# Moving score products into the feed-forward steps of a fused attention and feed-forward kernel

## The chip, the cores and the metric

The kernel runs on one core of a Trainium2 chip. The metric is device time in microseconds (us) of one execution; lower is better. The engines are PE (TensorE, matrix products; its weight loads are listed as PEld), DVE (VectorE), ACT (ScalarE), POOL (GpSimd) and SP (SyncE, which here only issues DMAs). Each engine runs its own list of instructions in order and waits on semaphores. TensorE's clock has two levels, 1.2 and 2.4 GHz; the profile gives the granted clock as a share of the full level, so 0.50 is the lower one.

## The reference

Eight batches of 256 rows by 512 columns pass through two blocks.

```
x = x + attention1(causal_conv(x))           # 16 heads of 32, causal, ALiBi; qkv 512 -> 1536
u = attention2(x)                            # cond2: the 512 columns are the positions, 256 rows the channels
    Q, K, V = W x ;  att = Q K / 4 + b       # 16 heads of 16, 512 x 512 scores a head, masked keys
    y = softmax(att) V
x = x + ffn(y)                               # gate, up 512 -> 2048, down 2048 -> 512
    inter = silu(y Wg) * (y Wu);  out = inter Wd
```

The feed-forward weights are Catmull-Rom splines of few control points. Everything is fp32; products that need it are split into a high and a low part that run through TensorE's faster fp32r path.

## The kernel before

The work is written out by hand as one ordered list for each engine; `batch(b)` appears in each of them, with counts of semaphores (`wait("name", n)`) between engines. Batch 0 stands alone, batches 1 to 6 are a hardware loop, batch 7 stands alone again, and the feed-forward part of the last batch follows by itself.

The feed-forward part of batch b-1 is carried inside batch b. A batch has these stages on PE: scores, softmax and values of attention1; its projection; the queries, keys and values of attention2 (L955, L960); the **feed-forward window**; the **loop over j** of attention2; then the next batch's first values (L835).

**Feed-forward window.** Eight steps n (`NT` = 8), each over 256 of the 2048 inner columns. PE does `moments(n+1)` (L846, y against a table, into bank 2 or 7), `gate_up(n)` (L857) and `down(n-1)` (L868 to L870, 12 products that accumulate in banks 5 and 6, its weights in a ring of `RING` = 3 buffers that SP refills with 1 MB DMAs, L269). ACT does `z_copy(n+1)` (L518), Silu (L529) and a rounded copy (L534). DVE does `gated(n)` (L662) and `rest(n)` (L667). `down(n)` needs `rest(n)`.

**Scores of attention2.** 64 products of 52 x 512 (L977, `scores(s)`), 16 for each of 4 groups of heads, alternate between banks 0 and 1. DVE takes the maximum of each row (L741, `maximum(s)`), and `scores(s)` waits for `maximum(s-2)`. After a group's 16 maxima, `turn(g)` transposes them on PE (L990), DVE negates and splits them (L748, L751), and `max_rows(g)` issues four small DMAs on ACT's queue (L568) that put them as extra rows into `q2`. Only then can the shifted scores of that group run. 24 scores are in the window (`WINDOW_SCORES`): four in each of steps 4 to 7, then eight behind step 7. Their order in a step:

```
PE   moments(n+1), two scores, gate_up(n), two scores, down(n-1)
DVE  gated(n), two maxima, rest(n), two maxima
```

`turn(0)` follows step 7. The operands of the scores, `stack2_g`, are written by 12 DMAs of 64 KB for each group (`stacks2(g)`, L351), between which SP also issues the ring's loads.

**Loop over j.** 35 steps. Step j does `shifted(j)` (L1009, two products of 54 x 512; exp on ACT follows, L592), two of the remaining 40 scores while j < 20, and `values2(j-3)` (L1021, eight products of 128 x 256 with 32 columns each). At `TURN_AT` (j = 4, 12, 20) comes `turn(g)`; at `OUT_AT` (11, 19, 27) `turn_outputs` (L1033), after ACT has brought a group's result out (L575); at `QK1_AT` (j = 20 to 27) eight products each (L829) for the next batch's queries and keys. `shifted(1)` waits for `totals` (L674, DVE adds the feed-forward result to the residual), because it writes a bank of that sum. `shifted(8g)` waits for `max_rows(g)`.

**Values of attention2.** V is left in banks 0, 1, 6 and 7 (L960); DVE copies it out (L734) behind the splitting of queries and keys. `moments(1)` and the first scores wait for these copies, since they use the same banks.

Of the kernel before, what the change touches and what calls it, by code (L numbers as in the profile page):

```python
# [59 lines left out]
WINDOW_FROM = 4  # L60
WINDOW_SCORES = 24
# [12 lines left out]
def window_scores(n):  # L74
    return max(0, min(GS, 4 * (n - WINDOW_FROM + 1))) if n < NT else WINDOW_SCORES

# [34 lines left out]
def block_program(nc, x_lanes, x_rows, taps, conv_b, qkv_wT, qk_b, v_b, out_wT, out_b, slopes, cond, w2T, att_b,  # L111
# [7 lines left out]
    with ExitStack() as ctx:  # L119
# [59 lines left out]
        d_rows = sb("wd_rows", [P, IT], I32)  # L179

# [61 lines left out]
        def _(sp):  # L242
# [22 lines left out]

# [54 lines left out]
            def batch(b, first=False, last=False):  # L320
# [39 lines left out]
                for g in range(NG):  # L360
                    stacks2(g)
                    for n in range(RING + g, RING + g + 1 if g < NG - 1 else NT):
                        if not first:
                            load_weights(b, n)
                    for n in (2 * g, 2 * g + 1):
                        if first:
# [132 lines left out]
        def _(act):  # L499
# [36 lines left out]
            def batch(b, first=False, last=False):  # L536
# [25 lines left out]
                def max_rows(g):  # L562
                    wait("max2_high", g + 1)
                    wait("max2_low", g + 1)
                    for i, part in enumerate((max2_h, max2_l)):
                        for e in range(2):
                            row = e * ROWS2 + MAX2 + i
                            act.dma_start(q2[row:row + 1, g, :, :].rearrange("p h (t n) -> p (h t) n", t=CT),  # L568
                                          part[e * 2 * CT:(e + 1) * 2 * CT, g % 2, :]).then_inc(S["max2_rows"], 16)
# [14 lines left out]
                max_rows(0)  # L584
                for j in range(NP):
# [11 lines left out]
                    if j in TURN_AT:  # L597
                        max_rows(TURN_AT.index(j) + 1)
# [18 lines left out]
        def _(dve):  # L617
# [59 lines left out]
            def batch(b, first=False, last=False):  # L677
# [39 lines left out]

                wait("mask_loaded", 48)
# [8 lines left out]

                if first:
                    dve.wait_ge(gate_up_step, 3 * N_GEN)
                    nc.vector.memset(v2[:], 1.0).then_inc(ones_made, 1)  # L730
                    dve.wait_ge(ones_made, 2)
# [36 lines left out]
                for n in range(NT):  # L768
                    if first:
# [3 lines left out]
                    else:  # L773
                        gated(b, n)
                    had, now = window_scores(n - 1), window_scores(n)
                    for s in range(had, (had + now) // 2):
                        maximum(s)
                    if not first:
                        rest(b, n)
                    for s in range((had + now) // 2, now):  # L780
                        maximum(s)
                turn(0)
                for s in range(GS, WINDOW_SCORES):
                    maximum(s)
# [39 lines left out]
        def _(pe):  # L824
# [14 lines left out]
            def moments(b, n):  # L839
# [21 lines left out]
            def down(b, n):  # L861
                pe.wait_ge(S[f"w_loaded_{n % RING}"], fed(b, f"w_loaded_{n % RING}", 16 * (n // RING + 1)))
                pe.wait_ge(S["inter_low"], fed(b, "inter_low", n + 1))
                for s in range(LT):
                    for g in range(2):
                        lhs = (slice(None), n % 2, g, slice(s * P, (s + 1) * P))
                        w_h, w_l = stack1[:, n % RING, 0, g, :], stack1[:, n % RING, 1, g, :]
                        nc.tensor.matmul(psum[:, SUM_BANK + s, :], r(inter_h[lhs]), r(w_h), start=n + g == 0, stop=False)  # L868
                        nc.tensor.matmul(psum[:, SUM_BANK + s, :], r(inter_h[lhs]), r(w_l), start=False, stop=False)  # L869
                        last = nc.tensor.matmul(psum[:, SUM_BANK + s, :], r(inter_l[lhs]), r(w_h), start=False,  # L870
                                                stop=n == NT - 1 and g == 1)
                last.then_inc(S["down_step"], 1)

            def batch(b, first=False, last_batch=False):
# [105 lines left out]
                def turn(g):  # L980
# [3 lines left out]
                    elif g == 0:  # L984
                        pe.wait_ge(S["z_out"], fed(b, "z_out", NT))
                    elif g == 1:
                        wait("max2_low", 1)
                    else:
                        wait("y_out", g - 1)
# [36 lines left out]
                def turn_outputs(g):  # L1026
                    wait("o2_out", g + 1)
                    if g < NG - 1:
                        wait("max2_low", g + 2)
# [6 lines left out]
                if first:  # L1036
                    pe.wait_ge(fixed2, 64)
                    for s in range(GS):
                        scores(s)
                    turn(0)  # L1040
                    for s in range(GS, WINDOW_SCORES):
                        scores(s)
                else:
# [3 lines left out]
                    for n in range(NT):  # L1047
                        had, now = window_scores(n - 1), window_scores(n)
                        if n == 0:
                            wait("v2_out", CT)  # L1050
                        if n + 1 < NT:
                            moments(b, n + 1)
                        for s in range(had, (had + now) // 2):
                            scores(s)
                        if n == 0:
                            wait("k2_out", LT)
                        gate_up(b, n)
                        for s in range((had + now) // 2, now):
                            scores(s)
                        if n:  # L1060
                            down(b, n - 1)
                    turn(0)
                    for s in range(GS, GS + 2):
                        scores(s)
                    down(b, NT - 1)
                    for s in range(GS + 2, WINDOW_SCORES):
                        scores(s)
# [51 lines left out]
            moments(B, 0)  # L1119
            for n in range(NT):  # L1120
                if n + 1 < NT:
                    moments(B, n + 1)
                gate_up(B, n)
                if n:
                    down(B, n - 1)
            down(B, NT - 1)
# [148 lines left out]
```

## Time and profile before

| | us |
|---|---|
| three runs | 1688.45, 1693.24, 1705.03 |
| median | 1693.24 |
| profiled execution, its own time | 1703.24 |
| span of the profiled execution | 1701.4 |

| engine | busy us | share of the span |
|---|---|---|
| PE | 1414.6 | 83% |
| PEld | 783.8 | 46% |
| DVE | 774.7 | 46% |
| ACT | 509.6 | 30% |
| POOL | 350.6 | 21% |

The mean granted clock of TensorE is 0.854 of full speed. A busy PE may be busy at the lower level, where the same product takes about twice as long. The device time of the profiled execution is 1.84 us more than its span.

### The profile page before, as it was taken

The page shows a single profiled execution, that of the slowest core. Times are in us where ns is not written, and L with a number is a line of the kernel's source. Part 1 is how long each engine was busy: PE and PEld are TensorE (multiplying, and loading weights), DVE is VectorE, ACT ScalarE, POOL GpSimd, SP SyncE. Part 2 cuts the span into 40 slices and gives each one's busy share as a digit, 9 for nine tenths or more (in the row PEclk, how much of TensorE's full clock was granted, in tenths as well). Part 3 has the DMA queues.
Part 4 walks back from the last instruction along what each step waited for, and adds up shares of the span by engine and source line. Part 5 has one row for each costly group of instructions (what it writes and reads, how often), then busy time and mean ns, then how long its engine had stood idle before and what let it go on. Part 6 is the DMA issues. An engine that isn't in the chain of part 4 may idle for free.

```text
span 1701.4 us, 23331 instructions
## 1 busy us (share of the span) xinstructions
PE 1414.6 (83%) x8680; PEld 783.8 (46%) x8680; DVE 774.7 (46%) x1205; ACT 509.6 (30%) x652; POOL 350.6 (21%) x203
## 2 busy tenths in 40 slices
PE   4571698888988899888988889888998889898988
PEld 3240245453555435454454534554355544555435
DVE  5344634446244553535435362544525354343622
ACT  2021253214412243222432135122432224331352
POOL 3289103410052100801026100521008010000000
PEclk9795599986898869986899869998699877998679
DMA  9767312550335303361034602353033610345203
GB/s 301 236 188 238 106 36 68 149 157 18 69 109 128 119 2 88 118 162 57 13 78 140 178 18 60 105 134 126 2 88 114 163 61 2 88 136 165 101 1 136
DMA packets 80495, 181.12 MB, mean 106 GB/s; under 512 B 14404, under 2 KB 54292, under 8 KB 70708
## 3 DMA queue, kind: packets, MB, share of 16 engines
q1 hardware_dynamic: 76304, 174.68, 35.1%
q0 software_dynamic: 1280, 4.20, 1.0%
q8 instruction: 82, 1.34, 0.3%
q10 hardware_dynamic: 2816, 0.79, 0.2%
q14 instruction: 13, 0.11, 0.0%
HBM read 106.41 MB, written 21.14 MB: 75 GB/s over the span
## 4 chain that ended last, share of the span: by engine, by line
PE 63%; DVE 14%; issue 6%; ACT 6%; POOL 4%; DMA 3%; ACTq 3%; SPq 1%; DVEq 0%; POOLq 0%
PE psum L1021 9%; PE psum L829 7%; PE psum L977 6%; PE psum L1009 6%; PE psum L868 5%; PE psum L870 4%; PE psum L869 4%; PE psum L857 3%; PE psum L846 3%; DVE max L741 3%; PE psum L835 3%; ACTq L568 3%; ACT probs L592 2%; PE psum L946 2%; PE psum L911 2%
## 5 line engine op out<-in xcount | busy, mean ns | idle before, releaser
L741 DVE TENSOR_REDUCE max<-psum 128x1 f32<-128x512 f32 x512 | 329.6, 685 | 121.7 <-PE psum L977 120.4
L592 ACT ACTIVATE probs<-psum 128x1024 f32<-128x1024 f32 x256 | 255.6, 1023 | 262.7 <-PE psum L1021 191.9
L977 PE MATMUL psum<-k,q 52*128 52x512 f32 x512 | 204.3, 580 | 117.3 <-DVE max L741 102.7
L1021 PE MATMUL psum<-probs,v 128*32 128x256 f32 x2048 | 205.7, 488 | 18.9 <-ACT o L575 14.0
L977 PEld LDWEIGHTS psum<-k,q 52*128 52x128 f32 x512 | 103.0, 243 | 202.5 <-DVE max L741 170.7
L1009 PE MATMUL psum<-q,k 54*128 54x512 f32 x512 | 168.7, 625 | 23.3 <-ACT probs L592 16.4
L662 DVE TENSOR_TENSOR probs<-psum,probs 128x512 f32<-128x512 f32 x64 | 44.3, 692 | 243.6 <-ACT probs L529 243.6
L829 PE MATMUL psum<-h,qkv_w 128*128 128x256 f32 x512 | 133.5, 408 | 18.2 <-DVE h L627 18.0
L479 POOL TENSOR_TENSOR h<-h_in,tap 128x1024 f32<-128x1024 f32 x7 | 13.3, 1901 | 643.6 <-PE psum L835 643.5
L1009 PEld LDWEIGHTS psum<-q,k 54*128 54x128 f32 x512 | 62.4, 231 | 150.8 <-issue 85.0
L868 PE MATMUL psum<-stack 128*128 128x512 f32 x256 | 123.1, 481 | 2.0 <-DVE stack L667 2.0
L489 POOL TENSOR_TENSOR h<-h,products 128x1024 f32<-128x1024 f32 x49 | 121.8, 2486 | 3.8
L829 PEld LDWEIGHTS psum<-h,qkv_w 128*128 128x128 f32 x512 | 98.1, 201 | 52.5 <-issue 25.3
L554 ACT ACTIVATE probs<-psum 128x1024 f32<-128x1024 f32 x64 | 62.2, 1022 | 196.2 <-PE psum L932 196.2
L870 PE MATMUL psum<-stack 128*128 128x512 f32 x256 | 115.7, 452 | 0.0
L869 PE MATMUL psum<-stack 128*128 128x512 f32 x256 | 115.1, 450 | 0.0
L486 POOL TENSOR_TENSOR products<-h_in,tap 128x1024 f32<-128x1024 f32 x49 | 99.2, 2025 | 3.0
L518 ACT ACTIVATE z<-psum 128x256 f32<-128x256 f32 x64 | 24.4, 381 | 233.2 <-PE psum L846 233.2
L1021 PEld LDWEIGHTS psum<-probs,v 128*32 128x32 f32 x2048 | 47.2, 121 | 101.8 <-issue 60.5
L846 PE MATMUL psum<-y,z_table 128*32 128x256 f32 x1024 | 73.2, 408 | 24.9 <-DVE v L734 24.1
L646 DVE CAST high<-low 128x1024 fp32r<-128x1024 f32 x32 | 26.6, 830 | 145.7 <-ACT low L505 109.5
L707 DVE RECIPROCAL inv<-psum 128x256 f32<-128x256 f32 x32 | 56.2, 1758 | 68.6 <-PE psum L911 67.8
(103 smaller groups left out, 1777.8 us busy)
## 6 DMA issues: line engine op xcount, KB each, us to landing
stack<-wd_sorted SPq DMA_DIRECT2D x64, 1024.0 KB, 5.9
stack<-high SPq DMA_DIRECT2D x128, 128.0 KB, 2.4
stack<-low SPq DMA_DIRECT2D x64, 128.0 KB, 2.4
q<-high SPq DMA_DIRECT2D x128, 64.0 KB, 4.7
k<-high SPq DMA_DIRECT2D x128, 64.0 KB, 2.6
wd_sorted<-stack SPq DMA_DIRECT2D x8, 1024.0 KB, 5.0
h_in<-in_x_lanes SPq DMA_DIRECT2D x9, 512.0 KB, 5.0
x<-in_x_rows SPq DMA_DIRECT2D x8, 512.0 KB, 5.6
```

Source lines behind the costliest of these rows:

```text
L486: nc.gpsimd.tensor_tensor(products[:], h_in[:, :, k:k + L], over(tap[:, :, k:k + 1]), ALU.mult)\
L489: nc.gpsimd.tensor_tensor(h[:], h[:], products[:], ALU.add).then_inc(S["conv_step"], 1)
L592: nc.scalar.activation(probs[:, u // 2 % 2, u % 2 * 2:u % 2 * 2 + 2, :], psum[:, 2 + u % 2 * 2:4 + u % 2 * 2, :], ACT.Exp)\
L741: nc.vector.reduce_max(max2[:, g, e, i, t:t + 1], psum[:, s % 2, :], AX_X).then_inc(S["s2_max"], 1)
L829: last = nc.tensor.matmul(psum[:, o % 2, 0:L], qkv_w[:, c, o * P:(o + 1) * P], h[:, c, :], start=c == 0, stop=c == CT - 1)
L846: last = nc.tensor.matmul(psum[s * ZR:(s + 1) * ZR, Z_BANKS[n % 2], 0:L], zt[:, c, cols], y[:, c, :], start=i == 0, stop=i == 1, skip_grou ...
L868: nc.tensor.matmul(psum[:, SUM_BANK + s, :], r(inter_h[lhs]), r(w_h), start=n + g == 0, stop=False)
L869: nc.tensor.matmul(psum[:, SUM_BANK + s, :], r(inter_h[lhs]), r(w_l), start=False, stop=False)
L870: last = nc.tensor.matmul(psum[:, SUM_BANK + s, :], r(inter_l[lhs]), r(w_h), start=False, stop=n == NT - 1 and g == 1)
L977: nc.tensor.matmul(psum[:, e, :], r(q2[rows, g, i, t * P:(t + 1) * P]), r(k2[rows, g, i, :]), start=True, stop=True).then_inc(S["s2_ready" ...
L1009: last = nc.tensor.matmul(psum[:, 2 + u % 2 * 2 + e, :], r(k2[rows, g, u % 2, kt * P:(kt + 1) * P]), r(q2[rows, g, u % 2, :]), start=True, ...
L1021: last = nc.tensor.matmul(psum[e * BLK:(e + 1) * BLK, 6, queries], v2[:, kt, head, :], probs[:, kt % 2, e, queries], start=kt + half == 0, ...
```

## The change

The scores move forward and change their place in a step. `WINDOW_FROM` goes from 4 to 1, and `WINDOW_SCORES` is now 4 x (8 + 1 - 1) = 32: four in each of steps 1 to 7 and four in a new step 8, which holds only `down(7)`. `down` is cut into its two halves of six products. In a step:

```
PE   moments(n+1), two scores, gate_up(n), [turn(0) at n = 5], down(n-1) half 0, two scores, down(n-1) half 1
DVE  two maxima, gated(n), [turn(0) at n = 5], two maxima, rest(n)
```

From these constants follow `TURN_AT` = 0, 8, 16 and `QK1_AT` = 16 to 23; `OUT_AT` stays. The loop keeps 32 scores, two a step while j < 16. `moments(7)` waits until `turn(0)` has been read out of bank 7.

`max_rows` goes from ACT's queue to SP's: group 0 behind the next mask's load, groups 1 to 3 behind the store of the output. SP now issues `stacks2(1)` before it waits to refill the ring, and then loads 3; 4 and 5; 6 and 7 behind groups 1, 2 and 3. V is copied out by ACT, in front of the feed-forward part, no longer by DVE. Two activations of one element each (`warm`) stand where they make ACT load its table: Silu ahead of the queries, Exp behind the feed-forward part. The memset of `v2` in batch 0 moves ahead of the splits.

```diff
-WINDOW_FROM = 4
-WINDOW_SCORES = 24
+WINDOW_FROM = 1
+WINDOW_SCORES = 4 * (NT + 1 - WINDOW_FROM)
+TURN_STEP = WINDOW_FROM + GS // 4
...
+def window_pair(n, i):
+    first = 4 * (n - WINDOW_FROM) + 2 * i
+    return range(first, first + 2) if n >= WINDOW_FROM else ()
...
+            def max_rows(b, g):
+                sp.wait_ge(S["max2_high"], at(b, "max2_high", g + 1))
+                sp.wait_ge(S["max2_low"], at(b, "max2_low", g + 1))
+                for i, part in enumerate((max2_h, max2_l)):
+                    for e in range(2):
+                        row = e * ROWS2 + MAX2 + i
+                        sp.dma_start(q2[row:row + 1, g, :, :].rearrange("p h (t n) -> p (h t) n", t=CT),
+                                     part[e * 2 * CT:(e + 1) * 2 * CT, g % 2, :]).then_inc(S["max2_rows"], 16)
...
-                    for n in range(RING + g, RING + g + 1 if g < NG - 1 else NT):
-                        if not first:
-                            load_weights(b, n)
+                    else:
+                        for n in ((), (3,), (4, 5), (6, 7))[g]:
+                            load_weights(b, n)
...
                     load_mask(cond[b])
+                max_rows(b, 0)
...
                     sp.dma_start(out[b - 1], x_res).then_inc(S["out_stored"], 16)
+                for g in range(1, NG):
+                    max_rows(b, g)
...
+                if not first:
+                    nc.scalar.activation(warm[:], ones[:, 0:1], ACT.Silu)
...
+                for t in range(CT):
+                    wait("v2_ready", t + 1)
+                    nc.scalar.activation(v2[:, t, :, 0:DH],
+                                         psum[:, V2_BANKS[t], 0:L].rearrange("p (h d) -> p h d", h=H2), ACT.Copy)\
+                        .then_inc(S["v2_out"], 1)
...
-                max_rows(0)
+                    nc.scalar.activation(warm[:], ones[:, 0:1], ACT.Exp)
...
-                    if j in TURN_AT:
-                        max_rows(TURN_AT.index(j) + 1)
...
-                for t in range(CT):
-                    wait("v2_ready", t + 1)
-                    nc.vector.tensor_copy(v2[:, t, :, 0:DH],
-                                          psum[:, V2_BANKS[t], 0:L].rearrange("p (h d) -> p h d", h=H2))\
-                        .then_inc(S["v2_out"], 1)
...
+                    for s in window_pair(n, 0):
+                        maximum(s)
+                    if not first and n < NT:
                         gated(b, n)
+                    if n == TURN_STEP:
+                        turn(0)
+                    for s in window_pair(n, 1):
                         maximum(s)
-                    if not first:
+                    if not first and n < NT:
                         rest(b, n)
...
+                if turned and n == TURN_STEP + 2:
+                    pe.wait_ge(S["max2_low"], at(b, "max2_low", 1))
...
+                for n in range(NT + 1):
+                    if not first and n + 1 < NT:
+                        moments(b, n + 1)
+                    for s in window_pair(n, 0):
+                        scores(s)
+                    if not first and n == 0:
+                        wait("k2_out", LT)
+                    if not first and n < NT:
                         gate_up(b, n)
+                    if n == TURN_STEP:
+                        turn(0)
+                    if not first and n:
+                        down(b, n - 1, 0)
+                    for s in window_pair(n, 1):
                         scores(s)
+                    if not first and n:
+                        down(b, n - 1, 1)
```

## Rows read from the trace of the kernel before

**Rows 1.** The page, parts 1 and 2: TensorE's busy time; granted clock in 40 slices.

```profile
PE 1414.6 (83%) x8680; PEld 783.8 (46%) x8680; DVE 774.7 (46%) x1205; ACT 509.6 (30%) x652; POOL 350.6 (21%) x203
...
PEclk9795599986898869986899869998699877998679
```

**Rows 2.** The page, part 4: the chain that ended last, by engine.

```profile
PE 63%; DVE 14%; issue 6%; ACT 6%; POOL 4%; DMA 3%; ACTq 3%; SPq 1%; DVEq 0%; POOLq 0%
```

**Rows 3.** Stretches of 4 us: length, busy PE PEld DVE ACT POOL, clock, DMA.

```profile
560.00:564.00 4.00, 4.00 (x33) 2.66 (x33) 0.63 (x2) 0.38 (x1) 0.00 (x0) 1.00 0.81 266
...
588.00:592.00 4.00, 3.51 (x10) 1.98 (x10) 3.71 (x7) 1.83 (x2) 0.00 (x0) 0.50 0.23 95
...
604.00:608.00 4.00, 4.00 (x26) 1.44 (x23) 2.52 (x4) 1.42 (x3) 0.00 (x0) 0.50 0.00 0
...
640.00:644.00 4.00, 4.00 (x29) 2.39 (x26) 0.00 (x0) 1.92 (x4) 0.00 (x0) 1.00 0.00 0
```

**Rows 4.** Timeline (start, length, engine, line): moments of two steps without scores.

```profile
532.74 1.07 PE L846 MATMUL psum<-y,z_table 128*32 128x256 f32 x16
...
537.75 1.07 PE L846 MATMUL psum<-y,z_table 128*32 128x256 f32 x16
```

**Rows 5.** Timeline of a step with four scores, up to the next one's.

```profile
554.90 0.50 PE L977 MATMUL psum<-k,q 52*128 52x512 f32 x2
...
557.55 1.28 DVE L741 TENSOR_REDUCE max<-psum 128x1 f32<-128x512 f32 x2
...
558.29 1.09 PE L977 MATMUL psum<-k,q 52*128 52x512 f32 x2 [2.02 <-DVE max L741]
...
563.23 0.50 PE L977 MATMUL psum<-k,q 52*128 52x512 f32 x2
```

**Rows 6.** Timeline where the feed-forward window begins.

```profile
521.75 1.41 DVE L734 COPY v<-psum 128x256 f32<-128x256 f32 x4
...
523.21 1.94 PE L846 MATMUL psum<-y,z_table 128*32 128x256 f32 x16 [4.02 <-DVE v L734]
...
525.61 1.28 ACT L529 ACT_TABLE_LOAD   x1
```

**Rows 7.** DMA view of 523 to 528 us: busy tenths in 40 slices.

```profile
DMA  9812199121000000000000000000000000000000
```

**Rows 8.** Timeline between the feed-forward window and the loop.

```profile
581.97 1.36 ACTq L568 DMA_DIRECT2D q<-max_h  x2
...
588.03 0.79 PE L1009 MATMUL psum<-q,k 54*128 54x512 f32 x2
...
590.36 0.80 PE L1009 MATMUL psum<-q,k 54*128 54x512 f32 x2 [0.49 <-DVE o L674]
```

**Rows 9.** Timeline of PE: shifted scores of loop steps that also have scores.

```profile
607.68 0.79 PE L1009 MATMUL psum<-q,k 54*128 54x512 f32 x2
...
609.84 0.79 PE L1009 MATMUL psum<-q,k 54*128 54x512 f32 x2
...
615.01 0.50 PE L1009 MATMUL psum<-q,k 54*128 54x512 f32 x2
...
618.12 0.51 PE L1009 MATMUL psum<-q,k 54*128 54x512 f32 x2
...
621.52 0.50 PE L1009 MATMUL psum<-q,k 54*128 54x512 f32 x2 [1.60 <-ACT probs L592]
```

**Rows 10.** Timeline of PE: first L829 of the loop, then its end.

```profile
635.89 3.62 PE L829 MATMUL psum<-h,qkv_w 128*128 128x256 f32 x8
...
660.30 0.50 PE L1009 MATMUL psum<-q,k 54*128 54x512 f32 x2
...
663.57 0.49 PE L1009 MATMUL psum<-q,k 54*128 54x512 f32 x2
...
667.55 0.66 PE L1033 MATMUL psum<-ident,o 128*128 128x128 f32 x4 [0.72 <-ACT o L575]
```

**Rows 11.** Timeline of SP: the last two loads of the ring.

```profile
558.13 4.52 SPq L269 DMA_DIRECT2D stack<-wd_sorted  x2
```

More of the change, by code:

```diff
@@ L179, in block_program @@
         d_rows = sb("wd_rows", [P, IT], I32)
+        warm = sb("warm", [P, 1])
         halves = probs[:, 1].rearrange("p e n -> p (e n)")
@@ L560, in batch @@
                         .then_inc(S["q2_out"], 1)
[L562 to L569, printed above, removed]
+                if first:
+                    act.wait_ge(ones_made, 2)
+                for t in range(CT):
[3 more added lines that the diff above has]
+                        .then_inc(S["v2_out"], 1)
                 def o2_evac(g):
@@ L716, in batch @@
                         .then_inc(S["x1_out"], 1)
+                if first:
+                    dve.wait_ge(gate_up_step, 3 * N_GEN)
+                    nc.vector.memset(v2[:], 1.0).then_inc(ones_made, 1)
                 wait("mask_loaded", 48)
@@ L766, in outputs @@
                         .then_inc(S["y_out"], 1)
-                for n in range(NT):
-                    if first:
+                for n in range(NT + 1):
+                    if first and n < NT:
                         dve.wait_ge(down_high, n + 1)
@@ L859, in gate_up, with down @@
                 last.then_inc(S["gu_ready"], 1)
[L861 to L872, printed above, removed]
+            def down(b, n, s):
+                if s == 0:
+                    pe.wait_ge(S[f"w_loaded_{n % RING}"], fed(b, f"w_loaded_{n % RING}", 16 * (n // RING + 1)))
+                    pe.wait_ge(S["inter_low"], fed(b, "inter_low", n + 1))
+                for g in range(2):
+                    lhs = (slice(None), n % 2, g, slice(s * P, (s + 1) * P))
+                    w_h, w_l = stack1[:, n % RING, 0, g, :], stack1[:, n % RING, 1, g, :]
+                    nc.tensor.matmul(psum[:, SUM_BANK + s, :], r(inter_h[lhs]), r(w_h), start=n + g == 0, stop=False)
+                    nc.tensor.matmul(psum[:, SUM_BANK + s, :], r(inter_h[lhs]), r(w_l), start=False, stop=False)
+                    last = nc.tensor.matmul(psum[:, SUM_BANK + s, :], r(inter_l[lhs]), r(w_h), start=False,
+                                            stop=n == NT - 1 and g == 1)
+                if s == LT - 1:
+                    last.then_inc(S["down_step"], 1)
             def batch(b, first=False, last_batch=False):
@@ L984, in turn @@
                     elif g == 0:
-                        pe.wait_ge(S["z_out"], fed(b, "z_out", NT))
-                    elif g == 1:
-                        wait("max2_low", 1)
+                        pe.wait_ge(S["z_out"], fed(b, "z_out", TURN_STEP + 1))
+                    elif g < NG - 1:
+                        wait("max2_low", g)
+                        if g == 1 and not first:
+                            pe.wait_ge(S["z_out"], fed(b, "z_out", NT))
                     else:
-                        wait("y_out", g - 1)
+                        wait("y_out", 1)
                     nc.tensor.transpose(psum[0:GH * CT, 7, 0:P], max2[:, g].rearrange("p e h t -> p (e h t)"), ident[:])\
@@ L1027, in turn_outputs @@
                     wait("o2_out", g + 1)
-                    if g < NG - 1:
-                        wait("max2_low", g + 2)
+                    if g < 2:
+                        wait("max2_low", g + 3)
                     else:
@@ L1037, in batch @@
                     pe.wait_ge(fixed2, 64)
[L1038 to L1042, printed above, removed]
                 else:
@@ L1046, in batch @@
                     moments(b, 0)
[L1047 to L1056, printed above, removed]
-                        gate_up(b, n)
[L1058 to L1063, printed above, removed]
+                    wait("v2_out", CT)
+                for n in range(NT + 1):
+                    if not first and n + 1 < NT:
[5 more added lines that the diff above has]
+                    if not first and n < NT:
+                        gate_up(b, n)
+                    if n == TURN_STEP:
[3 more added lines that the diff above has]
+                    for s in window_pair(n, 1):
                         scores(s)
-                    down(b, NT - 1)
-                    for s in range(GS + 2, WINDOW_SCORES):
-                        scores(s)
+                    if not first and n:
+                        down(b, n - 1, 1)
                 for j in range(NP + LAG):
@@ L1118, in _ @@
             pe.wait_ge(S["o2_out"], at(B - 1, "o2_out", NG))
-            moments(B, 0)
+            moments(B, 0, False)
             for n in range(NT):
                 if n + 1 < NT:
-                    moments(B, n + 1)
+                    moments(B, n + 1, False)
                 gate_up(B, n)
-                if n:
-                    down(B, n - 1)
-            down(B, NT - 1)
+                for s in range(LT if n else 0):
+                    down(B, n - 1, s)
+            for s in range(LT):
+                down(B, NT - 1, s)
 def spline_grid():
```

20 lines of the change are left out of this document (3 added, 17 removed).

## The prediction

> **What bounds the kernel now.** I read the page first. PE is busy 83% of the span and DVE 46% [rows 1], and the chain that ended last is PE in 63% and DVE in 14% [rows 2]. So PE sets the end, and two things can shorten it: idle time of PE, and time in which PE works at the lower clock. The granted clock has digits of 5 to 8 in many slices [rows 1]. The windows of 4 us of one batch then show where [rows 3]: at 560 (feed-forward window) PE is busy 4.00 of 4 us at clock 1.00; from 588 (loop) it is busy 3.51, later 4.00 of 4 us, at 0.50; at 640, with L829 in the loop, it is back at 1.00. Last I took the timeline of that batch, for what ended each pause of PE. Batches 1 to 7 repeat the pattern, one about every 199 us.
>
> **A. The beginning of the window.** PE pauses 4.02 us before `moments(1)`, for DVE's four copies of V, 1.41 us, which stand behind DVE's splitting [rows 6]. ACT is idle there, and takes V as PE delivers it; I cost the four copies at DVE's 1.41 us, beside PE's own products of V, and nothing on the path. ACT's 1.28 us table load [rows 6] moves to where ACT idles as well. If that cover failed, it would cost 1.3 us a batch once. `moments(0)` ended at 519.2, so `moments(1)`, `gate_up(0)` and `moments(2)`, each close to 1 us (moments are listed with 1.07) [rows 4], now end near 522.2 instead of beyond 527. But step 1 now begins with scores, and these need `stack2_0`. Its DMAs are not touched by the change; they are busy until a quarter of the stretch that begins at 523, so until 524.25 [rows 7]. The added wait is thus 522.2 to about 524.7, and behind it in PE's list stand `gate_up(1)` and both halves of `down(0)`; ACT and DVE wait for these. A pause of 4.02 us goes, one of 2.5 us comes.
>
> **B. The steps.** A step without scores takes 5.01 us [rows 4]. A step with four takes 8.33 us now (554.90 to 563.23), and the reason stands in it: the second pair of scores waits 2.02 us for maxima that DVE does after `gated` [rows 5]. In the new order the first maxima come before `gated`, and half a `down` lies between the pairs. PE needs 5.01 + 2 x 0.45 = 5.9 us a step (a pair is listed with 0.50 us [rows 5], its tail overlaps what follows). DVE needs four maxima, 2.56 us [rows 5], and `gated` and `rest` of the same width, some 1.3 us: 3.9 us, less than PE. `rest(n)` is now the last of DVE's list in a step, done some 4 us behind `gate_up(n)`; `down(n)` begins 5.9 us behind it, so it stays covered, and if it did not, each step would grow by what it is late. From the first pair at 524.7: six intervals of 5.9 (35.4), step 7 without moments (4.9), step 8 (a `down`, 5.01 - 1.07 - 1.0 = 2.9, and two pairs: 3.8), `turn(0)` 0.3, and 0.6 for step 8, where no `gate_up` covers `rest(7)`. That ends at 569.7. The clock fell behind each longer pause of PE in this batch; I take 1.5 us for one such fall behind the 2.5 us pause of A. So `shifted(0)` starts at 571.2. It now starts at 588.03, because `turn(0)`, the four DMAs on ACT's queue (from 581.97) and their landing lie before it [rows 8]; in the new order these are done during steps 5 to 8. **Gain of A and B: 16.8 us a batch**, with eight more scores done.
>
> **C. The loop up to its first L829.** It now takes 635.89 - 588.03 = 47.9 us for 20 steps [rows 8, 10]. A step at the lower level takes 2.16 us (607.68 to 609.84), one at the higher level 1.56 us (two from 615.01 to 618.12) [rows 9]. The first step takes 2.33 us, since `shifted(1)` waits for `totals` [rows 8]; this stays. `max_rows` on ACT's queue delays exp: 1.60 us of PE before 621.52 [rows 9]; this goes for groups 1 and 2, and its cover on SP is the time from j = 0 to 8, 8 to 16 and 16 to 24, at least 12 us each. Queued behind it on SP are the next batch's `stacks1`, whose data come only four steps after the last `turn`. What the trace of before does not show is the clock in this loop once the window before it is dense. The bounds are 15 steps at 1.56 = 23.4 and 15 at 2.16 = 32.4. PE keeps its pauses for `totals` and for the first maxima, and right there, at 588, the level fell and then stayed at 0.50 while PE was fully busy [rows 3]. I take this row as the nearest: the level falls again in the first steps and comes back after some 24 us, as it did. That gives 2.33 + 11 x 2.16 + 4 x 1.56 + 2.0 (one pause for `o2`, `turn(1)` and `turn(2)`, L1033) = 34.4 us for 16 steps. **Gain 13.5**; with the higher level throughout 20.1.
>
> **D. Steps with L829, and the bare steps.** The eight with L829 take 24.4 us [rows 10]. The first one's L829 is at the lower level, 3.62 us; at the higher one it takes about half: **gain 1.6** on either way. Then come eight bare steps instead of four. One takes 1.09 us (660.30 to 663.57 are three) [rows 10]: 4 x 1.09 = 4.4, and 1.6 for the second L1033 and its pause, which L829 hid before. **Loss 6.0.** This is where part of the loop's gain is given back.
>
> **Sum.** 16.8 + 13.5 + 1.6 - 6.0 = 25.9 us a batch, seven times: 181. Batch 0 has no feed-forward part: four steps fewer at 1.56 to 2.16, two delays of exp gone, two to three us earlier `max_rows`, less the 6.0: about 7. Together 188 us. The profiled execution's own time is 1703.24; it would become 1515. The median of the runs lies 10 us lower, at 1693.24, which by the same sum gives 1505. Between them I say 1510.
>
> **Rival 1: the higher level throughout the loop.** The window before the loop is dense, and ACT's issues no longer make pauses. Then the loop gains 20.1 instead of 13.5, and nothing falls in A (1.5): 34 a batch, about 33 with some pauses left, so 7 x 33 + 10 = 241 and a time of 1452 to 1462. For it: from 640 on PE is dense at 1.00. Against it: from 604 to 608 PE is just as dense, with 0.50 [rows 3].
> The Trainium skill (TensorE: Matmul & The Clock Gate, "Part 1: The HAM clock gate") has this case as its rule: the default is the throttled clock, and activity releases it. By it a loop in which PE never stops belongs at the higher level, and the time would be this rival's. The row at 604 disagrees: the products with 32 columns that fill it did not raise the level for over 15 us. That keeps the rival behind my forecast.
>
> **Rival 2: SP's queue is late.** SP must issue 36 DMAs of the stacks, five loads, the mask's and `max_rows(0)` in a window that ends 17 us earlier. Loads 6 and 7 are issued from 558.13 today [rows 11]; with `stacks2(1)` no longer behind `down(0)` they come at about 552 and 554, and `down(6)` wants the first near 561.5. By a landing of 6 to 7 us this is covered by 3 us only. If DMA engines, 0.81 busy at 560 [rows 3], stretch it, PE waits for 2 to 3 us in two steps, and the level may fall with each pause: some 10 us a batch, time 1575 to 1580.
>
> **Rival 3, slower.** In the window the level falls and doesn't come back, because scores of 52 rows and moments of 32 columns lie among the products of each step. A step at the lower level takes about twice 5.9, which adds some 5 us in each of eight steps, 40 a batch. Against a gain of 25.9 that is 14 lost: 7 x 14 = 98, about 1790. It decides once the lower level holds for more than two thirds of the window. Against it: dense steps ran at 1.00 at 560, scores included [rows 3].
>
> **Rival 4: the overlap doesn't come.** If PE still waits about 2 us for maxima in each step, as in rows 5, steps cost 8.3 us, the window gains nothing, and what is left is C and D and four steps less: about 9 to 10 a batch, 1630.
>
> **Chances.** Forecast 0.45, rival 1 0.28, rival 2 and smaller pauses like it 0.17, rival 4 0.05, rival 3 0.05. The range for 8 in 10 leaves out rivals 3 and 4 and a part of the rest: 1450 to 1580. Within 1% of the median, about what these runs can tell from no change, nothing of my cases lies except by chance: 0.02.
>
> **What would show it.** `DVE max` must no longer release L977 in the window, and successive L846 must be 5.9 us apart. Before the first scores PE should wait about 2.5 us for a DMA. `shifted(0)` should follow the last `down` at once, with no ACTq in the chain. The granted clock at the loop's start decides between forecast and rival 1, and idle time of L868 released by a DMA would be rival 2. The prediction is wrong if `rest` ends behind the second `gate_up`, or if the loop at the lower level lasts into the steps with L829 and the bare ones.

## The result and the profile after

The changed kernel takes 1526.56 us (median of four, 1524.18 to 1534.9), the kernel before beside it 1690.85: a ratio of 0.902, 95% interval 0.897 to 0.908. I had said 1510, from 1450 to 1580. The profiled execution has a span of 1524.4 us, 177.0 less than before.

The page, parts 1, 2 and 4, to be held against [rows 1] and [rows 2]:

```profile
PE 1337.0 (88%) x8680; PEld 733.3 (48%) x8680; DVE 773.8 (51%) x1173; ACT 524.4 (34%) x698; POOL 354.6 (23%) x203
...
PEclk9696589998799968999799999899899987999969
...
PE 67%; DVE 13%; POOL 5%; issue 4%; DMA 4%; ACT 4%; SPq 3%; DVEq 0%; ACTq 0%; POOLq 0%
```

With the same 8680 products PE is busy 77.6 us less: it spends less time at the lower clock. ACTq has left the chain (3% before, 0% now). In the changed kernel's lines moments are L854, scores L986, `gate_up` L865, `down` L876 to L878, the shifted scores L1020, `values2` L1032, and the maxima L749.

The timeline gives each stage of a batch between two starts on PE: the window (first moments to first shifted score), the scored part (to the first L829, now L835), the part with those products (to the last of them), and the bare part (to the last transposes of outputs). Means of batches 1 to 6, in us; the last column is the time at the lower clock in the whole execution.

| kernel | window | scored part | with L829 | bare part | lower clock |
|---|---|---|---|---|---|
| before | 69.97 | 47.16 | 23.57 | 7.56 | 498 |
| after | 51.97 | 34.79 | 23.02 | 14.68 | 324 |
| difference | -18.0 | -12.4 | -0.6 | +7.1 | |
| forecast | -16.8 | -13.5 | -1.6 | +6.0 | |

That is 23.8 us a batch, for 25.9 forecast. Batch 7 gives 25.1, batch 0 gives 8.9, and 6 x 23.8 + 25.1 + 8.9 = 177.

**The window.** Timeline of PE at its beginning, where moments(0) and (1) start at 491.95:

```profile
494.88 1.07 PE L854 MATMUL psum<-y,z_table 128*32 128x256 f32 x16
...
498.80 0.50 PE L986 MATMUL psum<-k,q 52*128 52x512 f32 x2 [2.85 <-DMA k<-low]
...
503.24 0.50 PE L986 MATMUL psum<-k,q 52*128 52x512 f32 x2
...
505.26 1.07 PE L854 MATMUL psum<-y,z_table 128*32 128x256 f32 x16
...
509.15 0.50 PE L986 MATMUL psum<-k,q 52*128 52x512 f32 x2
...
511.17 1.07 PE L854 MATMUL psum<-y,z_table 128*32 128x256 f32 x16
```

The 4.02 us pause of [rows 6] is gone, and a pause of 2.85 us for the first scores' DMA is there. From 505.26 to 511.17 a step takes 5.91 us, and the second pair at 509.15 waits for nothing, where [rows 5] had 2.02 us. Summed over a window of batches 1 to 6, PE waited about 9.1 us for maxima and 4.0 us for V before; now it waits 3.0 us for the DMA (mean) and never for a maximum.

**The loop.** Its head, timeline of PE, for [rows 8]:

```profile
543.88 0.40 PE L878 MATMUL psum<-stack 128*128 128x512 f32 x1
544.21 0.50 PE L1020 MATMUL psum<-q,k 54*128 54x512 f32 x2
...
545.82 0.50 PE L1020 MATMUL psum<-q,k 54*128 54x512 f32 x2 [0.67 <-DVE o L689]
```

`shifted(0)` follows the last `down` at once. Then stretches of 4 us (length, busy PE PEld DVE ACT POOL, clock, DMA), for [rows 3]:

```profile
540.00:544.00 4.00, 3.59 (x16) 2.28 (x14) 2.98 (x5) 0.00 (x0) 1.37 (x1) 1.00 0.00 0
544.00:548.00 4.00, 3.05 (x13) 1.08 (x11) 3.60 (x9) 2.18 (x3) 0.00 (x0) 0.91 0.48 143
548.00:552.00 4.00, 3.99 (x16) 1.63 (x16) 3.14 (x5) 1.91 (x2) 0.00 (x0) 0.50 0.14 37
...
576.00:580.00 4.00, 4.00 (x26) 1.51 (x24) 2.24 (x5) 1.94 (x2) 0.00 (x0) 0.50 0.00 0
```

The level is up in the window and falls 3.1 us behind the loop's start, in the head, where PE pauses for `totals` and maxima. From 552 to 568 PE is then busy 4.00 us in each stretch of 4 us, and the level stays down. In every one of batches 1 to 7 it falls 3.0 to 5.6 us behind the start. How long it stays down differs: 33.6, 34.7, 20.5, 6.8, 10.2 and 34.1 us in the scored parts of batches 1 to 6, which take 37.8, 37.8, 34.6, 29.8, 31.1 and 37.6 us. The Trainium skill (TensorE: Matmul & The Clock Gate, "Part 1: The HAM clock gate") says that activity releases the throttled clock. In the row at 576, as in [rows 3] at 604, PE never stops and the granted clock is 0.50, so a busy PE was not enough here.

### The profile page after: what moved, and what is told of

Read it like the earlier page. It is cut to its first block, busy times and chain, and to the rows that moved or that the text cites. A ratio compares the mean times of both kernels' runs of the same rounds, so it can differ in the third digit from the quotient of the medians.

```text
span 1524.4 us, 23370 instructions
## 1 busy us (share of the span) xinstructions
PE 1337.0 (88%) x8680; PEld 733.3 (48%) x8680; DVE 773.8 (51%) x1173; ACT 524.4 (34%) x698; POOL 354.6 (23%) x203
## 4 chain that ended last, share of the span: by engine, by line
PE 67%; DVE 13%; POOL 5%; issue 4%; DMA 4%; ACT 4%; SPq 3%; DVEq 0%; ACTq 0%; POOLq 0%
PE psum L1032 11%; PE psum L835 8%; PE psum L986 7%; PE psum L1020 7%; PE psum L876 5%; PE psum L877 4%; PE psum L878 4%; PE psum L865 3%; PE psum L841 3%; PE psum L854 3%; DVE low L663 2%; PE psum L955 2%; DVE max L749 2%; PE psum L920 2%; PE psum L937 2%
## 5 line engine op out<-in xcount | busy, mean ns | idle before, releaser
L749 DVE TENSOR_REDUCE max<-psum 128x1 f32<-128x512 f32 x512 | 329.8, 685 | 161.5 <-PE psum L986 159.5
L986 PE MATMUL psum<-k,q 52*128 52x512 f32 x512 | 173.7, 548 | 62.7 <-DVE max L749 30.9
L1032 PE MATMUL psum<-probs,v 128*32 128x256 f32 x2048 | 198.9, 475 | 22.5 <-ACT o L592 19.1
L1020 PE MATMUL psum<-q,k 54*128 54x512 f32 x512 | 157.8, 591 | 9.9 <-DVE o L689 4.7
L986 PEld LDWEIGHTS psum<-k,q 52*128 52x128 f32 x512 | 84.2, 224 | 145.3 <-DVE max L749 76.1
L835 PE MATMUL psum<-h,qkv_w 128*128 128x256 f32 x512 | 130.3, 401 | 18.0 <-DVE h L642 17.9
L835 PEld LDWEIGHTS psum<-h,qkv_w 128*128 128x128 f32 x512 | 96.0, 197 | 51.0 <-issue 24.6
L1020 PEld LDWEIGHTS psum<-q,k 54*128 54x128 f32 x512 | 57.9, 217 | 128.9 <-issue 88.4
L876 PE MATMUL psum<-stack 128*128 128x512 f32 x256 | 115.4, 451 | 2.0 <-DVE stack L682 1.8
L768 DVE RECIPROCAL inv<-psum 128x16 f32<-128x16 f32 x32 | 8.2, 258 | 192.8 <-PE psum L1044 192.8
L877 PE MATMUL psum<-stack 128*128 128x512 f32 x256 | 102.5, 400 | 0.0
L878 PE MATMUL psum<-stack 128*128 128x512 f32 x256 | 102.3, 400 | 0.0
L1032 PEld LDWEIGHTS psum<-probs,v 128*32 128x32 f32 x2048 | 47.2, 120 | 104.9 <-issue 61.7
L443 POOL TENSOR_TENSOR x<-x,out_bias 128x1024 f32<-128x1024 f32 x8 | 19.5, 2438 | 258.1 <-DMA x<-in_x_rows 258.1
L898 PE MATMUL psum<-stack 100*128 100x256 f32 x256 | 62.2, 327 | 9.9 <-DVE max L706 9.5
```

Source lines behind the costliest of these rows:

```text
L749: nc.vector.reduce_max(max2[:, g, e, i, t:t + 1], psum[:, s % 2, :], AX_X).then_inc(S["s2_max"], 1)
L835: last = nc.tensor.matmul(psum[:, o % 2, 0:L], qkv_w[:, c, o * P:(o + 1) * P], h[:, c, :], start=c == 0, stop=c == CT - 1)
L986: nc.tensor.matmul(psum[:, e, :], r(q2[rows, g, i, t * P:(t + 1) * P]), r(k2[rows, g, i, :]), start=True, stop=True).then_inc(S["s2_ready" ...
L1020: last = nc.tensor.matmul(psum[:, 2 + u % 2 * 2 + e, :], r(k2[rows, g, u % 2, kt * P:(kt + 1) * P]), r(q2[rows, g, u % 2, :]), start=True, ...
L1032: last = nc.tensor.matmul(psum[e * BLK:(e + 1) * BLK, 6, queries], v2[:, kt, head, :], probs[:, kt % 2, e, queries], start=kt + half == 0, ...
```

## The experiments

All times are medians; each ratio is against the kernel before on the same chip, whose median lay between 1691 and 1699 us, so that a difference of a few us between two experiments says nothing. The base is the changed kernel (ratio 0.902, interval 0.897 to 0.908) unless said otherwise. Stages are means of batches 1 to 6.

**1. The old order, with 32 scores.**

```diff
-                    if not first and n:
-                        down(b, n - 1, 0)
                     for s in window_pair(n, 1):
                         scores(s)
                     if not first and n:
+                        down(b, n - 1, 0)
                         down(b, n - 1, 1)
 # DVE: gated, pair, rest, pair
```

> The changed kernel with the old order within a step (PE: both halves of down behind the second pair; DVE: gated, pair, rest, pair) and still 32 scores from step 1 on. Theory order: each of seven steps waits 2 us or more for maxima again and takes 8.3 us and more; the window grows by 7 x 2.4 = 17 us or more and the time is 1527 + 7 x 17 = 1645 or more. Theory earliness: the window grows by less than 5 us a batch, below 1560.

Measured: 1719.95 us, ratio 1.015 (1.010 to 1.019): none of the gain is left, and the kernel is 1 to 2% above the one before. The window grew from 52.0 to 79.3 us, with 14.7 us of waiting for maxima in each. Timeline of one step:

```profile
556.95 1.07 PE L854 MATMUL psum<-y,z_table 128*32 128x256 f32 x16
...
561.33 1.09 PE L986 MATMUL psum<-k,q 52*128 52x512 f32 x2 [2.02 <-DVE max L749]
...
565.28 1.07 PE L854 MATMUL psum<-y,z_table 128*32 128x256 f32 x16
```

The step takes 8.33 us and has the 2.02 us wait, exactly as in [rows 5]. Spreading scores over more steps without the order multiplies the wait, and its pauses bring 24 us and more of the lower clock into each window. The theory of earliness falls: with `turn(0)` as early as in the change, the time is no better than before. The order carries the gain.

**2. The scores from step 3 on.** As many scores in the window as before (24), in the new order; the waits around bank 7 as in the kernel before.

```diff
-WINDOW_FROM = 1
+WINDOW_FROM = 3
...
```

> The changed kernel with the scores from step 3 on (24 in the window, as before the change), so that the new order within a step stands alone and the loop keeps 20 steps with scores. Theory order (the window's gain is the maxima out of PE's way): steps with scores stay at 5.9 us, the 2.85 us pause for the first scores' DMA goes, so moments(0) to shifted(0) takes about 52 - 3.4 (eight scores) - 3 = 46 us; the loop takes 4 scored steps more (6 to 9 us) and 4 bare ones fewer (6 us). About 1500 to 1525 us. Theory earliness (the gain is that turn(0) and its rows are done long before the loop): the window stays above 55 us and the time is 1560 or more.

Measured: 1483.46 us, ratio 0.875 (0.870 to 0.881), 43 us faster than the change itself and below both theories' ranges. Window 48.0, scored part 39.4 (20 steps), bare part 7.56; lower clock 190 us in all. Timeline of PE where its first scores come:

```profile
490.22 1.07 PE L854 MATMUL psum<-y,z_table 128*32 128x256 f32 x16
491.22 0.50 PE L986 MATMUL psum<-k,q 52*128 52x512 f32 x2
...
496.12 1.07 PE L854 MATMUL psum<-y,z_table 128*32 128x256 f32 x16
```

No DMA is waited for, and the step takes 5.90 us. The window gains 4 us: the pause is gone, eight scores are too (four pairs, 1.8 us at the prediction's 0.45 a pair), and `down` now waits 1.2 to 2.1 us a window for `rest` (L682), against 0 to 0.6 in the change. Scored plus bare part are 46.9 us against 49.5: although at the same clock the earlier start should win there (with fillers, below, 38.1 + 7.6 against 29.7 + 13.8), the level is down less. Starting at step 1 paid 4 us in the window and gained 2 us behind it at best.

**3. From step 2 on** (28 scores).

```diff
-WINDOW_FROM = 1
+WINDOW_FROM = 2
-                        pe.wait_ge(S["z_out"], fed(b, "z_out", TURN_STEP + 1))
+                        pe.wait_ge(S["z_out"], fed(b, "z_out", NT))
```

> The changed kernel with the scores from step 2 on (28 in the window). Its first scores come 5 us later, when their DMAs have landed. Theory pause: the 2.85 us pause and the 3.4 us at the lower clock behind it go, the window takes about 52 - 1.7 - 4.5 = 46 us, the loop 2 scored steps more and 2 bare ones fewer; about 1500 to 1515. Rival: the pause only moves to another place (the weights' ring, or rest behind the maxima), and the time stays within 0.5% of the changed kernel's 1527.

Measured: 1486.27 us (1472.72 to 1504.77), ratio 0.871 (0.863 to 0.879), the same as from step 3. Window 47.9 us: again the 4 us, here with only two pairs fewer. The time lies below the expected 1500 to 1515. Most of the pause is gone, but not all: the waits for `rest` and `gated` grew from about 0.3 us a window to 1.3.

**4. Fillers at the loop's head.** Eight extra products.

```diff
+                def filler(bank, count):
+                    for i in range(count):
+                        nc.tensor.matmul(psum[:, bank, 0:L], qkv_w[:, i % CT, 0:P], out_w[:, i % CT, 0:L],
+                                         start=True, stop=True, skip_group_check=True)
...
+                    if 0 < j < 4:
+                        filler(6, (3, 2, 2, 1)[j])
                     for s in range(WINDOW_SCORES + 2 * j, min(WINDOW_SCORES + 2 * j + 2, NS)):
                         scores(s)
...
+                    if j == 0:
+                        filler(4, 3)
```

> The changed kernel with eight products of 128 x 128 by 256 columns added (3 in bank 4 in loop step 0, then 2, 2, 1 in bank 6 in steps 1 to 3), where PE pauses for totals and for maxima. They are extra work and change no output. Theory pauses (the level falls 3 to 6 us behind the loop's start because PE pauses there, and how long it stays down sets the batch's time): the level stays at 1.00 in the scored steps, which then take 28 to 29 us instead of 30 to 38; about 1480. Theory kind (products of 32 columns cannot hold the level whatever PE does): the level falls some steps later, scored steps stay at 34 us and more, and the time is 1527 to 1535.

Measured: 1503.67 us (1500.74 to 1523.5), ratio 0.886 (0.881 to 0.890), 23 us faster though PE does more. The first three of a loop that starts at 535.04, timeline of PE (the trace lists each of these fp32 products twice):

```profile
535.82 1.46 PE L1006 MATMUL psum<-out_w,qkv_w 128*128 128x256 f32 x6
```

The same head in stretches of 4 us:

```profile
536.00:540.00 4.00, 4.00 (x19) 2.51 (x19) 2.93 (x7) 2.15 (x3) 0.00 (x0) 1.00 0.54 145
540.00:544.00 4.00, 4.00 (x23) 1.84 (x21) 3.10 (x5) 1.53 (x2) 0.00 (x0) 1.00 0.10 35
544.00:548.00 4.00, 4.00 (x36) 1.56 (x35) 3.38 (x6) 1.94 (x2) 0.00 (x0) 1.00 0.00 0
```

In four of six batches the level stays up through the whole scored part, which takes 29.7 us, as theory "pauses" had it; in the other two there are 13.1 and 3.4 us of the lower level. Theory "kind" falls: the same 32-column products behind a filled head run at 1.00. What the run doesn't separate is whether the level held because the pauses were gone or because eight products over all rows and columns stood in the head; fillers of another kind were not tried. I expected 1480. Of the missing 24 us some 19 are those two batches and the bare part: its mean is 15.7 us, and in five of six batches the level falls there, behind the pause for `o2`, where there is no filler.

**5. Fillers with scores from step 3**, and from step 2.

> Scores from step 3 on (1483 us as it stands, 8 to 14 us a batch of the lower level in its scored steps) with the same eight extra products at the head of the loop. Theory pauses: no lower level in the scored steps, 20 steps at 1.56 and the pauses, some 35 us instead of 39 to 40; about 1483 - 7 x 4.5 = 1450. Theory kind: the lower level stays at 10 us a batch, 1483 to 1490.

> Scores from step 2 on (28 in the window) with the eight extra products at the loop's head. Both theories held alone: the pause for the first scores gone (window 47.4 us), no lower level in the scored steps, which are 18: between 29.7 (16) and 38.1 (20), so 33.8; bare part 11.6, or 13 to 15 where the level falls there. About 1486 - 4 = 1475 to 1480, and at most 0.5% from the kernel with 24 scores and the fillers (1479), since a scored step and a bare one less cost the same.

Measured: 1479.07 us, ratio 0.873 (0.869 to 0.878), and 1471.38 us, ratio 0.866 (0.861 to 0.870). Granted clock of the first in 40 slices:

```profile
PEclk9697589999999999999999999999999999999999
```

In batches 1 to 7 of that kernel the loop has no lower level at all, and its scored part takes 38.1 us in each. It was expected to reach 1450 and didn't: the twenty steps at 1.00 take 38.1, not 35, only 1.3 us less than without fillers. The lower clock in all fell from 190 to 100 us, but its interval still overlaps that of experiment 2. The kernel from step 2 with fillers has the lowest median made here, a little below what was expected; in three of its six scored parts there are still 3.4 to 6.8 us of the lower level. Its interval touches or overlaps those of experiments 2 and 3 and of the other kernel here, so which of the four is fastest is not shown.

**6. The maxima's rows on ACT's queue.**

```diff
-                max_rows(b, 0)                      # SP
...
+                max_rows(0)                         # ACT, behind the feed-forward part
...
+                    if j in TURN_AT:
+                        max_rows(TURN_AT.index(j) + 1)
```

> The changed kernel with the maxima's rows issued on ACT's queue again, at the places that the change leaves for them (group 0 behind the feed-forward part, groups 1 to 3 behind turn). Theory issue (each group holds ACT for 2.6 us): exp is late by some 1.6 us in two or three places, 3 to 5 us a batch, and each such pause can cost the higher clock: 1550 to 1580. Rival (in the longer distances ACT has time): within 0.5% of 1527.

Measured: 1549.59 us, ratio 0.915 (0.909 to 0.921): 23 us slower than the change, just below the expected range. One line each of the timelines of ACT's queue and of PE:

```profile
561.12 1.29 ACTq L582 DMA_DIRECT2D q<-max_h  x2
```

```profile
564.98 0.50 PE L1020 MATMUL psum<-q,k 54*128 54x512 f32 x2 [1.58 <-ACT probs L607]
```

PE waits 1.58 us behind the issue of group 2, and 1.84 us behind that of group 1; over a whole loop its shifted scores wait 3.7 to 4.0 us for exp in batches 1 to 6, against 0.2 to 0.4 in the change. Even so these batches take no longer in the profiled execution (124.5 us in both kernels), since the lower level happened to last less in their scored parts, 19 us against 23. That execution is 12 us above the change's, from batches 0 and 7: in batch 7's loop there are 44.4 us of the lower level, where the change has 34.1. So the waits are shown; how the other executions come to 20 us and more is not, as only the shortest of the four (1537.9 us) was profiled.

**7. V copied out by DVE.** The four copies behind `split(b, 1, ...)` again.

> The changed kernel with V copied out by DVE again, behind its splits. Theory hidden (the 4.0 us pause before moments(1) only changed into the 2.85 us pause before the first scores, so the copies on ACT are worth little while these scores wait for their DMA): moments(1) at 5.1 us behind moments(0), the first scores 4 us later than now at most, about 2.5 to 3 us a batch and 1545 us. Theory full (4 us a batch and the level that goes with the pause): 1555 and more. Theory nothing: within 0.5% of 1527.

Measured: 1549.87 us (1523.83 to 1561.3), ratio 0.917 (0.912 to 0.921). That ratio is of little use: the two shortest executions, 1523.83 and 1537.47 us, are about 0.902 of the kernel before, like the change, and the three others (1549.87 to 1561.3) have a lower granted clock, 0.868 to 0.881 against 0.909 in the shortest. So no difference in time is shown. The profile is that of the shortest execution, timeline of PE:

```profile
497.44 1.68 PE L855 MATMUL psum<-y,z_table 128*32 128x256 f32 x16 [4.03 <-DVE v L743]
```

The 4.03 us pause is back, and the one for the first scores' DMA is gone; the window takes 54.3 us against 52.0. So the copies on ACT are worth 2.3 us a batch in the window, and not the 4 us that the pause measured: theory "hidden".

**8. The order nearly alone**: from step 3, rows on ACT's queue, V by DVE (the edits of 2, 6 and 7 together).

> Close to the kernel before with the new order within a step alone: 24 scores from step 3 on, the maxima's rows on ACT's queue, V copied out by DVE. Of the change there stay the order, the ring loads behind stacks2(1) and the two table loads moved. Against 1483 us with the other parts. Theory additive: the 4 us pause before moments(1) and its level come back (window 47.4 + 4 to 6), ACT's issues cost the loop 4 to 6 us as in the kernel with them on ACT: 1483 + 7 x 9 = 1546, and of the 170 us that the change brought the order alone brings some 150. Theory earliness: with turn(0) only at step 7 its rows come 2 to 4 us late for the loop; 1570 and more.

Measured: 1556.33 us, ratio 0.917 (0.911 to 0.922), between the two theories. Against the kernel before that is 143 us for the order with its ring loads and table loads; against experiment 2 the two moved jobs are worth 73 us. Taken back one by one in the change they showed 23 us (experiment 6) and nothing clear (experiment 7); why they are worth more here was not tested. Window 52.6, scored part 44.2, against 48.0 and 39.4 in experiment 2.

**9. SP's old order of the ring's loads.**

```diff
-                        for n in ((), (3,), (4, 5), (6, 7))[g]:
+                        for n in range(RING + g, RING + g + 1 if g < NG - 1 else NT):
                             load_weights(b, n)
```

> The changed kernel with SP's old order of the ring's loads: load 3 behind stacks2(0), 4, 5, and 6 and 7 behind groups 1, 2 and 3, so that stacks2(1) waits for down(0). Theory late: stacks2(3) then ends some 10 us later, loads 6 and 7 are issued at about the time that down(6) wants them, PE waits 2 to 4 us for the DMA in one or two steps and the level may fall: 1540 to 1560. Rival (SP has room): within 0.5% of 1527.

Measured: 1523.79 us, ratio 0.897 (0.892 to 0.902), not to be told from the change. Timeline of SP, the last two loads of a window in this kernel, whose first moments are at 485.80:

```profile
524.60 0.99 SPq L282 DMA_DIRECT2D stack<-wd_sorted  x2
```

That is 38.8 us behind the first moments, against 33.4 in the change (525.30 and 491.95), and 0.3 us is all that L876 waited for a load between 480 and 560. My rival of a late queue was wrong by its cover: SP has 5 us to spare.

**10. Without the two table-loading activations.**

> The changed kernel without the two one-element activations, so that ACT loads its tables just before the first Silu and the first Exp. I costed this at nothing: the first Silu may be 1.3 us late, but the first down begins behind the 2.85 us pause; the first exp of the loop 1.3 us late, in which PE's list has scores that wait for maxima anyway. Theory hidden: 1520 to 1535. Theory exposed: 1.3 us twice a batch, 1545.

Measured: 1534.34 us, ratio 0.902 (0.897 to 0.907). Not to be told from the change: theory "hidden".

**11. The kernel before with the fillers alone.**

> The kernel before with only the eight extra products at the head of its loop (3 in bank 4 in step 0, then 2, 2, 1 in bank 6). Theory pauses: the scored steps, 47.8 us with 37.6 us of the lower level now, start at the higher one; ACT's issues then make a pause of 1.6 us twice, and the level may fall there. With the level up throughout, 20 steps take 38.1 us as in the kernel with 24 scores and the fillers, plus 2 x 1.6: 41.3, about 1698 - 7 x 6 = 1655. If it falls at the first of ACT's pauses, 45 us and 1680. Theory kind: the window before is not dense here, the level falls all the same, and the time is 1693 to 1705.

Measured: 1717.89 us, ratio 1.016 (1.008 to 1.023): no gain and probably a small loss, which neither theory had. The first three fillers in the timeline of PE, of a loop that starts at 593.44, and two stretches of 4 us:

```profile
594.84 2.67 PE L995 MATMUL psum<-out_w,qkv_w 128*128 128x256 f32 x6
```

```profile
592.00:596.00 4.00, 3.59 (x10) 1.94 (x11) 4.00 (x7) 1.02 (x1) 0.00 (x0) 0.89 0.13 16
596.00:600.00 4.00, 4.00 (x14) 2.11 (x12) 0.81 (x3) 1.02 (x1) 0.00 (x0) 0.68 0.32 131
```

The level falls here 0 to 2 us behind the loop's start, where the window has just ended with pauses, so the fillers come too late: the first three take 2.67 us instead of 1.46. The scored parts have 20 to 35 us of the lower level, where the kernel before has 27 to 38, so the fillers do some good; but in the loop shown a pause of 1.63 us for ACT ends at 610.50, and from 612 to 616 the granted clock is 0.53 again. In these kernels fillers held a level that was up and did little to raise one that was down.

## Why the prediction was right, point by point

**A, the beginning of the window: right.** The pause of 4.02 us turned into one of 2.85 for `k<-low` (2.5 forecast), and in batch 2 3.4 us of the lower clock followed. In experiments 2 and 3 the window without it is 4 us shorter, of which 1.8 and 0.9 us are the pairs of scores that left it (at 0.45 a pair). I had costed the pause as a remnant of a gain and not asked whether the first scores might simply start a step later.

**B, the steps: right.** 5.91 us for 5.9, no wait for maxima, no load late, and in most steps `rest` ends 0.9 us before the next `gate_up`. Experiment 1 shows that it is the order that does this. The gain of A and B was 18.0 for 16.8.

**C, the scored part: right on the mean, which is in part luck.** The size is a draw in each batch. I took it from the row at 588 that the level falls again and stays down for about 24 us, and forecast 34.4; the mean is 34.8. Single batches lie between 29.8, which is near rival 1's value of 27.7, and 37.8, a little more than my sum with 15 steps at 2.16 (2.33 + 32.4 + 2.0 = 36.7). The fall was as forecast. Experiment 4 takes it away with fillers in the head, which speaks for the pauses there as its cause, with the reserve made there; why the level comes back after 7 us in one batch and 35 us in another was not found. My reading of the row at 604 went too far: its steps hold products with 54 and 52 rows as well, so it could not show that the 32-column products were what kept the level down.

**D: two terms mis-sized.** The bare part grew by 7.1 us for 6.0, since the level fell there in two of six batches: 13.83 us without a fall is +6.3. The part with L829 gained 0.6 for 1.6: two batches enter it at the lower level, and two of the six of before had not. This is half of what I had named as a sign of being wrong, the lower level lasting into the steps with L829 and the bare ones: it lasts 2.8 and 4.0 us into the former in batches 1 and 2, and what the bare steps have is a new fall in batches 1 and 4.

**The sum** was 188 us for 177: 2.1 us a batch too much. D alone accounts for 2.1; A and B gave 1.2 more than forecast and C 1.1 less, which cancels. Rival 1 nearly held in one batch of six (29.8 us); experiment 4 shows that it was within reach, though at 29.7 us a scored part and not 27.7. Rival 2's mechanism did not occur and had room left (experiment 9). Rivals 3 and 4 did not occur, but experiment 1 is rival 4's kernel, and what I gave for it was wrong: I had 1630, on the ground that the window would then gain nothing, and 1720 was measured, because the waits now come in seven steps instead of four. In its profiled execution (1707.7 us) the window takes 9.4 us more than before and the loop 9.2 us less, so nothing is left of C.

What stays open: how much of the 177 us is the clock. In the scored parts 33.6 us of the lower level go with 8.1 us more than no lower level (37.82 against 29.74 in the kernel with fillers), 0.24 us each. At that price the 174 us of the lower level that are gone would be 42 us; `down` pays more (a product takes 628 ns at the lower level and 389 at the higher one), so this is an estimate from below.

## What to carry to other kernels

Where two engines pass results back and forth in a step, put the short exchange in front of the other engine's long job, and half of your own long job behind it; only then is it worth putting more of it into each step. An exchange that is spread without this multiplies its wait. Start moved work when its operands have landed, not as early as the order allows: one step later made this kernel 40 us faster, a quarter of the whole change again; 4 us a batch of it are in the window, the rest is in the loop, where the level is a draw. And look at the granted clock just behind a dense stretch: here the level fell at a few short pauses and stayed down for 7 to 35 us, and extra products in them paid only where the level was still up.

## What the runs showed of the hardware that I had not expected

TensorE stayed at the lower level (0.50) for up to 35 us of a scored part. From 552 to 568 us of the changed kernel its busy time was 4.00 of 4 us in each of the four stretches, in a loop of 52- and 54-row products and 32-column products. With eight extra products in the head and scores from step 3 on (experiment 5), the loop ran at 1.00 for its whole length in every batch from 1 to 7 (scored part 38.1 us in each of six batches). So products of the same kinds ran at either level for long.

A microsecond at the lower level cost these loops much less than half a microsecond: 0.24 us by the two scored parts above, and 0.28 by the prediction's steps (1.56 us for 2.16). DVE's two maxima take 1.28 us of a step at either level; that they and the exchange with ACT are what limits a step at 1.00 was not tested.
